# An even stream of maxima, row copies ahead of operand loads, and all sixteen items written out

## The reference

```python
qkv = (x @ qkv_w + qkv_b)                                  # q, k, v per head
std_logits = einsum('bhqd,bhkd->bhqk', q, k) * dh ** -0.5
read_lines, write_lines = exterior(r1, r2), exterior(w1, w2)   # 6 numbers per head and token
geo_logits = einsum('bqhi,bkhi->bhqk', read_lines, J_write) * inc_scale
std_out = softmax(causal(std_logits)) @ v
geo_out = softmax(causal(geo_logits)) @ geo_v
combined = (1 - gate) * std_out + gate * geo_out
x = layernorm(x + combined @ out_w + out_b)
x = layernorm(x + ffn(x))                                  # silu(gate) * up, 768 hidden
```

## Time and profile before

| | |
|---|---|
| median of three runs | 1957.65 us |
| profiled execution | 1961.9 us, span 1960.2 us |
| PE busy | 1693.0 us, 86% of the span |
| ACT busy | 1230.1 us, 63% |
| DVE busy | 1083.8 us, 55% |
| POOL busy | 337.4 us, 17% |
| mean granted clock of PE | 0.934 of full |
| first and last exponential of `attend` | 280.5 and 1609.6 us |

### The profile page before, as it was taken

How to read it: one execution, slowest core, us unless ns; L and a number is a source line. 1 busy time by engine, 2 the same in 40 slices (tenths; PEclk the granted TensorE clock), 3 DMA queues, 4 the chain that set the end, 5 groups by cost and what they waited for, 6 DMA issues and landing times. The chain is left out here.

```text
span 1960.2 us, 36600 instructions
## 1 busy us (share of the span) xinstructions
PE 1693.0 (86%) x11809; PEld 601.8 (31%) x11809; DVE 1083.8 (55%) x2557; ACT 1230.1 (63%) x1457; POOL 337.4 (17%) x479
## 2 busy tenths in 40 slices
PE   7986469989898999988989888988989874999998
PEld 4554112222222222222212222222222213565555
DVE  4774566655566566555656555665656502545432
ACT  3553318877787778778868777887778871211221
POOL 4332401112111011110102111011111112211100
PEclk9998559999999999899989999999899996999999
DMA  5764412021110111101111110101102004223000
GB/s 174 215 206 139 160 70 90 34 76 46 70 72 36 65 41 54 72 31 72 43 66 44 53 72 33 71 37 55 65 35 67 18 9 163 70 79 105 20 21 22
DMA packets 97412, 140.76 MB, mean 72 GB/s; under 512 B 8144, under 2 KB 66320, under 8 KB 95152
## 3 DMA queue, kind: packets, MB, share of 16 engines
q1 hardware_dynamic: 96000, 135.08, 20.2%
q0 software_dynamic: 624, 2.75, 0.4%
q10 hardware_dynamic: 576, 0.28, 0.1%
HBM read 81.96 MB, written 55.61 MB: 70 GB/s over the span
## 5 line engine op out<-in xcount | busy, mean ns | idle before, releaser
L1145 ACT ACTIVATE prob<-ex 128x1024 f32<-128x1024 f32 (+1 forms) x1152 | 1061.5, 977 | 315.8 <-PE ex L973 234.1
L1164 DVE TENSOR_REDUCE mp<-mx 128x1 f32<-128x512 f32 x768 | 492.3, 686 | 321.4 <-PE mx L1008 302.2
L1062 PE MATMUL pv<-prob,va 128*32 128x512 f32 (+3 forms) x5120 | 594.0, 556 | 0.5 <-POOL prob L945 0.5
L945 POOL TENSOR_SCALAR_AFFINE_SELECT prob<-prob 128x256 f32<-128x256 f32 (+1 forms) x384 | 187.1, 487 | 1172.9 <-ACT prob L1145 1169.2
L979 PE MATMUL ex<-dq,dk 34*128 34x512 bf16 (+7 forms) x2560 | 356.1, 360 | 23.2 <-ACT prob L1145 19.9
L1008 PE MATMUL mx<-dk,dq 64*128 64x512 bf16 (+3 forms) x1280 | 276.0, 370 | 68.8 <-DVE mp L1161 35.3
L1161 DVE CUSTOM_DVE_ANT_0 dull<-mx,mask_qk 128x128 f32<-128x128 f32 (+3 forms) x512 | 232.9, 489 | 140.1 <-PE mx L1008 137.7
L973 PE MATMUL ex<-gq,gk 38*128 38x512 bf16 (+3 forms) x1280 | 227.3, 367 | 65.3 <-DMA dq<-mrow 40.3
L973 PEld LDWEIGHTS ex<-gq,gk 38*128 38x128 bf16 x1280 | 57.9, 94 | 483.8 <-ACT prob L1145 367.6
L1062 PEld LDWEIGHTS pv<-prob,va 128*32 128x32 f32 x5120 | 117.0, 111 | 252.3 <-issue 218.3
L1495 ACT ACTIVATE sg<-pg 128x512 f32<-128x512 f32 x48 | 28.7, 597 | 245.8 <-PE pg L1435 240.2
(11 more groups left out here) (98 smaller groups left out, 905.4 us busy)
## 6 DMA issues: line engine op xcount, KB each, us to landing
values<-vn SPq DMA_DIRECT2D x32, 512.0 KB, 5.2
va<-values SPq DMA_DIRECT2D x16, 1024.0 KB, 13.6
raw<-on SPq DMA_DIRECT2D x64, 256.0 KB
parts_dot<-sp SPq DMA_DIRECT2D x32, 384.0 KB, 5.0
dq<-parts_dot SPq DMA_DIRECT2D x96, 128.0 KB
dk<-parts_dot SPq DMA_DIRECT2D x96, 128.0 KB
att<-raw SPq DMA_DIRECT2D x32, 256.0 KB
rr<-rden SPq DMA_DIRECT2D x32, 256.0 KB
```

Of the source, the lines that this page charges most:

```text
L945: g.affine_select(out=cut, in_=cut, compare_op=ALU.is_ge, fill=0.0, base=0, pattern=[[0, nb], [1, P]], channel_multiplier=-1).then_inc(mas ...
L1062: last = pe.matmul(pv[blk * VW:(blk + 1) * VW, CH - w:CH], sets[which]["v"][:, kb, blk * VW:(blk + 1) * VW], prob[UNIT_AT[s, j, kind] % NP ...
L1145: act.activation(prob[n % NPROB][:, :].rearrange("p (b c) -> p b c", b=2)[:, :, 0:w], ex[:, n % 2, :].rearrange("p (b c) -> p b c", b=2)[: ...
L1164: return v.tensor_reduce(out=to, in_=source, axis=AX.X, op=ALU.max)
```

## The change

Four things change, all in `attend` and its plan.

1. `max_places` gives another order. Before, up to three diagonal pairs shared a slot: three in slot 10 (128, 256, 384 keys) and slot 31, two in slots 28 and 29. Now slots 13, 16, 24, 27, 32 and 5 have two pairs (128 with 384, 256 with 256, and in slot 5 256 with 512), and every other slot but the turns has one.
2. In a slot with two pairs, one is computed between the geo and the dot scores, and the other behind the dot scores.
3. SP issues the LATE rows, and the store of column 1 behind them, ahead of loads 6 to 11.
4. PE, ACT, DVE and POOL have all sixteen items written out; `set_of` and the loops go.

The values computed are the same.

```diff
-    early = [cuts(0, 0, 1, 2), cuts(0, 3)] + fulls(1) + [cuts(1, 3)] + fulls(2)[0:2] + [cuts(1, 2), cuts(2, 2)]
-    early += fulls(2)[2:] + [cuts(2, 3), cuts(1, 0, 1), cuts(2, 0, 1)]
-    late = [cuts(3, 0, 1, 2)] + fulls(3) + [cuts(3, 3)]
+    early = [f for qt in (1, 2) for f in fulls(qt)] + [cuts(qt, 3) for qt in (0, 1, 2)] + [cuts(2, 1)]
+    late = fulls(3)
+    both = {13: cuts(0, 0, 2), 16: cuts(1, 0, 2), 24: cuts(2, 0, 2), 27: cuts(0, 1) + cuts(1, 1),
+            32: cuts(3, 0, 2), 5: cuts(3, 1, 3)}
...
                 load(range(0, 6))
                 store(it, 0)
+                rows(it, LATE, sets[it % NSET])
+                store(it, 1)
                 load(range(6, 12))
...
-                rows(it, LATE, sets[it % NSET])
-                store(it, 1)
                 load(range(12, 18))
...
-            with g.Fori(len(ffn) + 1, ITEMS) as it:
+            for it in range(len(ffn) + 1, ITEMS):
                 item(it, False)
...
                     scores(it, which, s, j, GEO, head)
                     if to:
-                        for u in MAX_IN[h]:
+                        for u in MAX_IN[h][:1]:
                             max_pair(it, to, u)
                     scores(it, which, s, j, DOT, head)
+                    if to:
+                        for u in MAX_IN[h][1:]:
+                            max_pair(it, to, u)
...
-            with pe.Fori(0, ITEMS // NSET - 1) as k:
-                for i in range(NSET):
-                    item(set_of(k, i), (NSET * k + i, i, k), set_of(k, i + 1), False)
-            for it in range(ITEMS - 3, ITEMS):
+            for it in range(1, ITEMS):
                 item(static(it), static(it - 1), static(it + 1) if it < LAST_ITEM else None, False)
...
-            with act.Fori(1, ITEMS) as it:
+            for it in range(1, ITEMS):
                 item(it, False)
...
-            with v.Fori(1, PAIRS_OF_HEADS) as it:
-                item(it, False, True)
-            item(PAIRS_OF_HEADS, False, True)
-            with v.Fori(PAIRS_OF_HEADS + 1, ITEMS - 1) as it:
+            for it in range(1, ITEMS - 1):
                 item(it, False, True)
```

More of the change, by code:

```diff
@@ L137, in fulls @@
         return [[by[qb, k0]] for qb in range(TT * qt, TT * qt + TT) for k0 in range(0, CH * qt, CH)]
-    early = [cuts(0, 0, 1, 2), cuts(0, 3)] + fulls(1) + [cuts(1, 3)] + fulls(2)[0:2] + [cuts(1, 2), cuts(2, 2)]
-    early += fulls(2)[2:] + [cuts(2, 3), cuts(1, 0, 1), cuts(2, 0, 1)]
-    late = [cuts(3, 0, 1, 2)] + fulls(3) + [cuts(3, 3)]
+    early = [f for qt in (1, 2) for f in fulls(qt)] + [cuts(qt, 3) for qt in (0, 1, 2)] + [cuts(2, 1)]
+    late = fulls(3)
+    both = {13: cuts(0, 0, 2), 16: cuts(1, 0, 2), 24: cuts(2, 0, 2), 27: cuts(0, 1) + cuts(1, 1),
+            32: cuts(3, 0, 2), 5: cuts(3, 1, 3)}
     out = [[] for _ in range(NPV)]
     for part, mine in ((EARLY, early), (LATE, late)):
[L144 to L148, removed]
+        at = [h % NPV for h in range(TURN[1 - part] + 1, TURN[1 - part] + NPV) if h % NPV != TURN[part]]
+        at = at[:next(n for n, h in enumerate(at) if (TURN[part] - h) % NPV == 1) + 1]
+        mine = mine[:]
+        for h in at:
+            out[h] = both[h] if h in both else mine.pop(0)
+        assert not mine
+        assert sorted(u for h in at for u in out[h]) == PART_TILES[part]
     return out
@@ L204, in item_of @@
     return it + 1 if part == EARLY else it
-def set_of(k, i):
-    return NSET * k + 1 + i, (1 + i) % NSET, k + (1 + i) // NSET
 def build(nc, xt, x, w_qk, b_qk, w_v, w_line, b_v, b_gate, inc, out_w, out_b, wg, wu, wd, out):
```

## The result

The changed kernel took **1854.07 us**, the median of four runs (1850.26 to 1856.87), beside 1957.7 us for the kernel before: a ratio of 0.947, with a 95% interval of 0.945 to 0.950. It is faster, as forecast, but it takes 44 us more than the 1810 of the forecast, and lies 4 us outside the range. The profiled execution has a span of 1852.8 us, at a mean granted clock of 0.952.

The account below looks back on a forecast made before the run. ACT's exponentials were the clock, with PE near full and losses in slots 20 to 23, 0 to 4, 35 and those with several pairs. 51.3 + 37.5 + 67.7 - 9.1 = 147.4 us off 1961.9, less 4.25, gave 1810; range 1794 to 1850.

Parts of the forecast that it names:

- the part on the row copies: Slots 20 to 23: LATE rows issued earlier end the whole wait and the low clock, 51.3 us less, bounds 0 and 51.3.
- Two pairs in a slot: Slots 5, 13, 16, 24, 27, 32: a second pair costs 0.1 us in each of 91 slots, 9.1 us more.
- Rival B: Slots with two pairs: the second pair still waits for its bank, 58.2 us in place of 9.1, 1859; chance 0.09.
- Rival A: Start of items: the next item's early rows land too late, 1 to 2 us in thirteen items, 1823 to 1836; chance 0.15.
- Slot 35: End of items: without PE's jumps back, slot 35 takes 2.53 us everywhere, 7.6 us less.
- second-order waits in slots 12 and 14: Waits in slots 12, 14 and 16 that might shrink, a few us, counted only in the forecast's lower end of 1795.
- slots 0 to 4: Start of items 1 to 15: with DVE written out they take 9.63 us each, 29.9 us less.
- rival D: Slots 20 to 23 do not wait for the rows, so 51.3 us stay, 1861; chance 0.06.
- C: Written-out code gives nothing because straight code stalls too, DVE above all: 37.5 us stay, 1848; chance 0.14.
- its harder form: Jumps over the `If` bodies stall at new places, 30 at 2.9 us on PE, 1897; chance 0.03, within C's.
- Slots 10, 28, 29 and 31: With one pair each they become ordinary slots: 27.0, 19.2 and 21.5 us less, together 67.7.
- E: SP's hold at the LATE rows idles the queue, so early rows come late: slower than before, 1993; chance 0.04.

Follow-up runs that it names:

- e1: Changed kernel with the loads of the denominators in item 8 issued ahead of the store of column 0 and the LATE rows: 1836.81 us.
- e2: Changed kernel with VectorE's inverse of the denominators five steps later in item 8, behind slot 28 in place of 19, no DMA moved: 1836.88 us.
- e7: Changed kernel with both pairs of maxima of a slot computed ahead of the dot scores: 1878.85 us.
- e3: Changed kernel with each operand load issued as two DMAs, one for each of its two leading slices: 1794.67 us.
- e14: Changed kernel with the operand loads of items 0 and 1 alone issued as two DMAs each: 1823.74 us.
- e12: Kernel before the change with all sixteen items written out on the four engines and nothing else changed: 1933.06 us.
- e6: Changed kernel with the LATE rows and the store of column 1 behind loads 6 to 11 again: 1916.7 us.
- e4: Changed kernel with VectorE's two loops back (items 1 to 7 and 9 to 14), all else written out: 1857.56 us.
- e9: Kernel with every operand load issued as two DMAs (e3), with VectorE's two loops back: 1798.46 us.
- e5: Changed kernel with TensorE's loop back (items 1 to 12, three per turn), all else written out: 1861.93 us.

## Why the prediction was wrong

**The step that failed** stands in the part on the row copies: "What is late next is nothing in these slots: item 14 shows them with the rows in time." What I listed behind the waiting SP was "the store of column 1 and eighteen loads". In item 8 the loads of the denominators stand there too, between loads 11 and 12, and VectorE waits for them behind the maxima of slot 19, which makes slot 21 long (19.92 us in place of 1.82). Item 14 could not show it. Nor was the 19.86 us of item 8 before, the largest of the table, a wait for rows alone: VectorE stood 6.43 us for `den_gate` in it, and I credited all of its excess to the rows. After the change the same stand was 14.59 us. In place of -51.3 the slots gave -31.7: 19.6 us, the largest miss. e1 and e2 show the cause, and each takes 17.2 to 17.3 us off.

**Two pairs in a slot** cost 22.8 us, and slot 30 3.1 more, in place of 9.1: 16.8 us. For the six slots the mechanism was right: the wait for the bank is gone (e7 brings it back, and costs 25 us). The size was not. Slot 30 I had at nothing, without looking at it. I took 0.1 us between bounds of 0 and 0.64 because five of the six slots hold 512 keys in both pairs, as a wide pair does. TensorE's busy time was the row to size it by. In slots 13 to 19 of item 2 it is busy for all 13.93 us, so each further product lengthens the slot. Measured against one wide pair it is 0.27 to 0.40 us. Rival B's mechanism did not occur.

**Rival A happened beside the forecast.** I counted the landing of the early rows at 70 to 73 us into an item of 73, gave it 0.15, and left it out of the sum. Slot 35 went +4.5 in place of -7.6: 12.1 us. The transfer had no slack, so the likely case already held some of it. e3 and e14 show the queue as its cause: with the loads spread inside `attend` too, every slot 35 takes 2.52.

**Given back the other way:** 9.3 us in the rest of `attend`. I had named second-order waits in slots 12 and 14 as possible and left them out of the sum; these gave 2.1. The run with nothing but written-out code (e12) has 9.6 in the rest, so the term belongs to that part, which I had counted in slots 0 to 4 and 35 alone. `finish` takes 1.7 more. 19.6 + 16.8 + 12.1 + 1.7 - 9.3 = 40.9 us; the rest of the sum was off by -0.9. That makes 40 us for the profiled executions (span 107.4 shorter, 147.4 forecast). For the medians it is 44: I took off the 4.25 us by which the profiled execution before lay above its median, and the changed kernel's lies only 0.4 above.

**What held.** LATE rows are issued 19 to 27 us into the items and slots 20 to 23 take 8.31 (rival D is out; e6). Slots 0 to 4 take 9.55 in every item but 0 and 3, and no branch stalls inside items (C and its harder form are out in the trace). Slots 10, 28, 29 and 31 came out within 0.5 us, in part by luck: 9.7 us of these came from the written-out code and not from the stream (e12). SP's hold left no idle queue (E is out).

**The parts do not add.** Undone one at a time, the rows are worth 63 us and the stream 15; done alone, writing out is worth 24. My terms were 51, 59 and 37. The wait ahead of slot 21 swallows what is gained ahead of it as long as the rows are late, and the early rows do the same once they are not.

## What to carry to other kernels

When a wait moves forward in a queue, list everything issued behind it for every item, the item with an extra step above all, and look at which engine waits for each. A stretch that is longest in one item deserves its own reading before its excess is credited to a common cause: here one more look at VectorE in item 8 would have shown the 6.43 us. If the forecast makes a stage shorter than a transfer that has no gap, put that transfer's end into the sum and not among the rivals; and here the transfer itself had more to give than its place in the queue: cutting each operand load in two took 59 us more off.

## What the runs showed of the hardware

- **An operand load cut in two.** Cutting the leading dimension of 2 off the loads raised the busy share of the DMA engines from 0.13 (593 to 596 us, item 4) to 0.61 (556.5 to 559.5 us in e3, the same place in the item), started `attend` 28 us earlier and took the rest of both late waits away (e3, e14).
- **A jump back has no fixed price.** VectorE's first reduction was 2.9 to 3.0 us late in items 11 to 14 of the kernel before and 0.2 to 1.1 in e4 and e9. At TensorE's three jumps slot 35 was 2.2 to 2.9 us longer than 2.53, before and in e5.
- **A gap costs twice.** In item 8 TensorE stood 16.27 us. In the 9.3 us behind that the granted clock was 0.50, and the two wide products of a pair took 0.64 us, where they took 0.38 ahead of the stand. In e1, with no such stand, the mean over the whole item is 1.00.
